# Dense sums of layers 2 and 3: three bf16 parts as one product of 512 columns and one of 256

## The reference, cut to what matters

```python
def _L1_gnn_ref(x, W1, b1, W2, b2, edge_index):
    loops = jnp.arange(n, dtype=edge_index.dtype)
    src = jnp.concatenate([edge_index[0], loops])
    dst = jnp.concatenate([edge_index[1], loops])
    deg = jax.ops.segment_sum(jnp.ones(src.shape[0], x.dtype), dst, num_segments=n)
    norm = dinv[src] * dinv[dst]                  # dinv = 1 / sqrt(deg)

    def gcn_conv(h, W, b):
        m = (h @ W)[src] * norm[:, None]
        return jax.ops.segment_sum(m, dst, num_segments=n) + b
    x1 = gcn_conv(x, W1, b1)
    x1 = x1 / jnp.maximum(jnp.linalg.norm(x1, axis=-1, keepdims=True), 1e-12)
    x2 = gcn_conv(x1, W2, b2)
    return x2 + x
```

## Time and profile before

| | us |
|---|---|
| median of 3 runs | 5319.24 |
| lowest and highest of them | 5316.11, 5332.93 |
| span of the profiled execution | 5305.9 |
| TensorE busy in it | 3977.3 (75%) |
| VectorE busy | 2919.9 (55%) |
| GpSimd busy | 2859.7 (54%) |
| ScalarE busy | 1417.2 (27%) |

### The profile page before, as it was taken

The page is one execution under the profiler, slowest core; times in us unless marked ns, Lnnn a source line. Parts: engine busy times, 40 slices in busy tenths (PEclk is TensorE's granted clock), DMA queues, the critical chain, the costliest instruction groups (busy, mean ns, idle before and its releaser), DMA issues.

```text
span 5305.9 us, 64097 instructions
## 1 busy us (share of the span) xinstructions
PE 3977.3 (75%) x20960; PEld 3151.6 (59%) x20961; DVE 2919.9 (55%) x7680; ACT 1417.2 (27%) x3894; POOL 2859.7 (54%) x3104
## 2 busy tenths in 40 slices
PE   6775655454555576777777996899996898886999
PEld 6653434343434455666666665787785777764666
DVE  7755655455546775555656556776665332243344
ACT  6603323232331222222222331333331000033221
POOL 7745566666656665565653002566565666643322
PEclk9857776777777777777777998999998999997999
DMA  3332343333333232222322002444444554444321
GB/s 92 106 70 78 110 112 100 98 99 99 97 95 90 86 87 79 81 85 81 86 81 66 25 14 74 130 144 144 138 146 140 160 155 138 138 136 135 103 80 54
DMA packets 337524, 535.23 MB, mean 101 GB/s; under 512 B 91587, under 2 KB 246452, under 8 KB 337186
## 3 DMA queue, kind: packets, MB, share of 16 engines
q0 software_dynamic: 133168, 361.15, 24.1%
q1 hardware_dynamic: 196902, 163.10, 10.0%
q10 hardware_dynamic: 7118, 6.83, 0.4%
HBM read 439.58 MB, written 94.26 MB: 101 GB/s over the span
## 4 chain that ended last, share of the span: by engine, by line
PE 54%; DVE 19%; issue 11%; another core or an unknown queue 11%; ACT 2%; DVEq 1%; POOL 1%; DMA 0%; ACTq 0%; SPq 0%; POOLq 0%
PE PSA L1091 15%; PE PSA L1239 12%; PE PSA L1486 4%; PE PSA L1472 4%; PE PSA L1248 4%; DVE ACC L2102 3%; PE PSA L1373 3%; PE PSA L1389 3%; DVE XIN L2075 2%; DVE XT L2075 2%; PE PSA L1041 1%; PE PSA L1219 1%; ACT ACC L1536 1%; DVE PSA L2066 1%
## 5 line engine op out<-in xcount | busy, mean ns | idle before, releaser
L915 POOL DMA_INDIRECT WORK<-tab,SRC x2504 | 2411.9, 963 | 1923.8 <-issue 666.6
L2102 DVE TENSOR_TENSOR ACC<-ACC,PSA 64x256 f32 x1296 | 541.9, 418 | 1221.2 <-remote 686.6
L1091 PE MATMUL PSA<-WORK,XIN 128*128 128x256 f32 x3032 | 881.2, 443 | 362.7 <-ACT XIN L1569 156.8
L1091 PEld LDWEIGHTS PSA<-WORK,XIN 128*128 128x128 f32 x3032 | 653.7, 225 | 490.5 <-issue 387.9
L1091 PE MATMUL PSA<-WORK,XT 128*128 128x256 f32 x1976 | 581.2, 446 | 217.8 <-ACT XT L1569 131.9
L1091 PEld LDWEIGHTS PSA<-WORK,XT 128*128 128x128 f32 x1976 | 427.7, 226 | 302.6 <-issue 226.4
L1239 PE MATMUL PSA<-WORK 128*128 128x256 bf16 x2730 | 367.0, 278 | 16.7 <-issue 16.5
L1239 PEld LDWEIGHTS PSA<-WORK 128*128 128x128 bf16 x2730 | 270.1, 100 | 60.7 <-issue 24.7
L2075 DVE TENSOR_TENSOR XIN<-PSA,DST 128x512 f32<-128x512 f32 x392 | 265.3, 679 | 3.9 <-issue 1.9
L1729 ACT ACTIVATE WORK<-PSA 128x512 bf16<-128x512 f32 x245 | 146.4, 598 | 428.1 <-PE PSA L1219 328.4
L1639 ACT ACTIVATE XIN<-XIN,HSB 128x128 f32<-128x128 f32 x504 | 160.2, 392 | 359.7 <-DVE XIN L2075 231.5
(11 more groups left out here) (511 smaller groups left out, 6768.4 us busy)
## 6 DMA issues: line engine op xcount, KB each, us to landing
WORK<-tab,SRC POOLq DMA_INDIRECT x2504
unit_counts_d<-WORK SPq DMA_DIRECT2D x245, 128.0 KB
WAX<-unit_counts_d SPq DMA_DIRECT2D x140, 128.0 KB
ACC<-in_L_ffn_w SPq DMA_DIRECT2D x16, 1024.0 KB
WORK<-unit_counts_d SPq DMA_DIRECT2D x105, 128.0 KB
tab<-WORK SPq DMA_DIRECT2D x98, 128.0 KB
slots_x<-FILL SPq DMA_DIRECT2D x4, 2080.0 KB
ACC<-slots_x SPq DMA_DIRECT2D x8, 910.0 KB
```

The lines of the kernel that those rows point to most:

```text
L915: po.indirect_dma_start(out=rows[:, 0:width], out_offset=None, in_=tab[:, :], in_offset=bass.IndirectOffsetOnAxis(ap=SRC[:, c:c + 1].bitca ...
L1091: last = pe.matmul(PS[h][:, 0:D], chosen[:, j * P:(j + 1) * P], rows[:, 0:D], start=(j == 0), stop=(j == Q - 1))
L2102: return ve.tensor_tensor(rows, rows, PS[h][half, 0:D], ALU.add)
```

## The change

`UNS` now names whole banks of 512 columns. In `sum_unit` the first two parts of a half, which stand side by side in SBUF (512 columns), are multiplied by one product into the whole bank, and the third part by a product of 256 columns that is summed onto the bank's first half. So a half takes two products in place of three, and the sums of a tile lie in two halves of a bank: parts 0 and 2 in the first, part 1 in the second. `add_tile` adds the second half to `ACC`, waits for that (`step` signals VectorE's own semaphore and `settle` waits for it), and then adds the first half.

```diff
-        UNS = [[PS[2][:, 0:D], PS[b][:, 0:D]] for b in (6, 5)]
+        UNS = [[PS[2], PS[b]] for b in (6, 5)]
...
-        def part_of(k, c):
-            first, held = [(t, v) for pieces in PIECES for t, n, _, v in pieces if t <= k < t + n][0]
-            return held[:, (k - first) * PD + c * D // 2:(k - first) * PD + (c + 1) * D // 2].bitcast(bf16)
+        def parts_of(k, c, n):
+            first, held = [(t, v) for pieces in PIECES for t, m, _, v in pieces if t <= k < t + m][0]
+            return held[:, (k - first) * PD + c * D // 2:(k - first) * PD + (c + n) * D // 2].bitcast(bf16)
...
                     for h in range(2):
-                        for c in range(C3):
-                            part = (v - 2 * n) * 2 + h
-                            last = pe.matmul(UNS[i][t % 2], UNC[i][n % len(UNC[i])][:, part * P:(part + 1) * P],
-                                             part_of(2 * u + h, c), start=(u == 0 and h == 0 and c == 0),
-                                             stop=(u == NL - 1 and h == 1 and c == C3 - 1))
+                        part = (v - 2 * n) * 2 + h
+                        counts = UNC[i][n % len(UNC[i])][:, part * P:(part + 1) * P]
+                        pe.matmul(UNS[i][t % 2], counts, parts_of(2 * u + h, 0, 2), start=(u == 0 and h == 0), stop=False)
+                        last = pe.matmul(UNS[i][t % 2][:, 0:D], counts, parts_of(2 * u + h, 2, 1), start=False,
+                                         stop=(u == NL - 1 and h == 1))
                 last.then_inc(s_ud, 1)
...
                 ve.wait_ge(s_ud, UNITS * i + last_unit(t) + 1)
-                ve.tensor_tensor(sums(t), sums(t), UNS[i][t % 2], ALU.add).then_inc(s_ut, 1)
+                step(ve.tensor_tensor(sums(t), sums(t), UNS[i][t % 2][:, D:2 * D], ALU.add))
+                settle()
+                ve.tensor_tensor(sums(t), sums(t), UNS[i][t % 2][:, 0:D], ALU.add).then_inc(s_ut, 1)
                 ve.wait_ge(s_ut, NT * i + t + 1)
```

## The result

The changed kernel takes 5375.84 us (median of 5 runs, 5338.59 to 5388.50), the kernel before beside it 5316.11 (5 runs): a ratio of 1.0101, 95% interval 1.0071 to 1.0131. I had forecast 5283 us. The profiled execution has a span of 5373.3 us, 67.4 us more than before's 5305.9.

A forecast was written before the change was run, and what follows sets the result against it. TensorE was taken to set the pace in layers 2 and 3. Columns -3.6, layer 3 stalls -34 and VectorE +1 summed to -36.6 us, giving 5283 us (chance 42%); the 8-in-10 range was 5230 to 5330 us.

The forecast's parts named there:

- The first step: Layers 2 and 3: TensorE, busy 650 of 725 and 585 of 655 us, sets the pace, so shortening its stream pays.
- it follows a TensorE that is up to 100 us faster: GpSimd in layer 3: its gathers wait 126 us for TensorE's side, so it would keep up with a faster TensorE.
- Columns: Dense sums, both layers: 1960 fewer products, 216.3 ns per 512 columns against two of 109.2 ns; taken as -3.6 us.
- Stalls of layer 3: TensorE in layer 3: fewer instructions remove 36% of 68.6 us of stalls and of 26 us lost clock; -34 us.
- instructions that arrive too slowly: Layer 3's dense products: supposed cause of TensorE's idle bursts without a semaphore, eight instructions arriving in 1.43 us.
- every instruction has the same chance: Layer 3: assumption that any TensorE instruction equally likely meets slow supply, leaving a share of 0.76 with fewer instructions.
- VectorE: Second addition in `add_tile`, about 0.5 us a tile, hidden by VectorE's waiting except at each layer's end; +1 us.
- the rival that made it late: Layer 2: the second addition delays one-hots for TensorE, costing 24.5 us, with layer 3's stalls unchanged; 5341 us, chance 6%.
- Layer 2's should move by 2 us or less: Expected sign: layer 2's stretch changes by at most 2 us, with TensorE's waits ahead of the count products unchanged.
- the 61 waits: Layer 2: 61 of 245 units followed by a count-product wait for copy or one-hot, losing a quarter of 2.05 us.
- The bursts move into layer 2 as well: Layer 2 catches stalls like layer 3's, costing 61 us, while layer 3 keeps its own; 5378 us, chance 7%.
- The stalls stay: Layer 3's stalls depend on time or other traffic, not instruction count; -2.6 us in all, 5317 us, chance 32%.

The follow-up runs named there:

- e8: Kernel before, with each gather of layers 2 and 3 replaced by a plain load of the same bytes from the same queue: 5123.18 us, ratio 0.9644.
- e15: Changed kernel with thirty small fills on GpSimd ahead of each group of four gathers in layer 2: 5296.67 us, ratio 0.9972.
- e16: Kernel before, with the third part's product of 256 columns split into two of 128, so four products a half: 5364.91 us, ratio 1.0112.
- e3: Changed kernel without VectorE's addition of the bank's second half, so the second part's sum is left out: 5359.25 us, ratio 1.0083.
- e4: Kernel before's three products of 256 columns, the second part's going into the bank's second half, with the changed kernel's two additions: 5322.07 us, ratio 1.0006.
- e13: Changed kernel, with the third part's product of 256 columns split into two of 128, so three products a half: 5301.19 us, ratio 0.9993.

## Why the prediction was wrong

**What sets the pace.** The first step failed: "in both layers TensorE sets the pace". TensorE's busy time of 90% does not show that. Without gathers (`e8`) the same TensorE stream runs layer 3 from its first dense product to its last in 549 us, where before took 662; and with more work on GpSimd (`e15`) the changed kernel got faster. I read the 126 us of GpSimd's waits as slack, "it follows a TensorE that is up to 100 us faster". They are pauses of a loop: GpSimd waits for TensorE's completions, and these often come late while gathers are out.

**Columns.** The size was right: 216 ns for 512 columns, 109 for the third part. With plain loads the two kernels take the same time.

**Stalls of layer 3.** The term -34 us is the one that carried the forecast, and it failed twice. The cause was not instructions that arrive too slowly (`e8`: none left, same pieces). And "every instruction has the same chance" does not hold: "issue" went from 68.6 to 67.0 us. Layer 3 did get shorter, by 10.2 us, and its clock rose to 0.98. That goes with longer rows of gathers (51 rather than 38 of seven or more) and fewer pauses; that the rows are the cause in this layer was not tested. The number of products does bear on this layer, since more of them cost 36 us (`e16`), but not by fewer waits named "issue".

**VectorE.** Right, and the rival that made it late fell. TensorE did wait longer for the one-hots, its sign, but without the second addition the loss stays (`e3`), and with the additions alone the ratio is 1.0006 (`e4`).

**Layer 2.** "Layer 2's should move by 2 us or less, with its waits ahead of L1219 unchanged" failed: it moved by 71 us, and the waits for the copy grew from 12.1 to 40.9 us. What the runs showed in its place is the loop of gathers and late completions, thrown out of its rhythm by two products a half in place of three. The hint stood in the earlier trace rows: waits of up to 4.7 us for ScalarE's copy, on an engine busy for 245 of 725 us, cannot come from the copy itself. I counted these waits and did not ask what the copy waited for. And 52 of the 61 waits that I put down to the copy or a one-hot end with "issue" in the earlier trace rows, 29.4 us: layer 2 stood still without a semaphore as well, only ahead of another product, so the two layers differed less than I thought.

**The rivals.** "The bursts move into layer 2 as well", at 7%, gave 5378 us and is nearest to 5376, but by another way: layer 3 did not keep its length, the waits named "issue" in layer 2 did not grow ahead of L1219 (29.4 to 27.0 us) and came to 0.9 us ahead of the dense products, and its price was borrowed from layer 3's. What it had right is that the two layers run the same products and that 1960 fewer could shift what follows. "The stalls stay" was right that fewer instructions leave the stalls of layer 3 as they are; they go with the gathers (`e8`). Its total was wrong, since it assumed a layer 2 that doesn't react.

**What stays open.** By which way the gathers hold up TensorE's completions, and whether TensorE also computes late then or only reports late, no run shows. That two products a half lengthen layer 2's rows of gathers is shown by `e13` against the changed kernel, and that these rows carry the loss by `e15`; why just two do so is not.

## What to carry over

An engine that is busy for 90% of a stretch need not set its pace. Where two engines wait for each other in turn, the waits are part of the pace and not slack: replace one side's work by something cheap (as in `e8`) before pricing a saving on the other. A saving on one side can lengthen the loop (after), and a pause on the other can shorten it (`e15`). A wait that ends with "remote" on a one-core kernel is a question: look at when the product was over and who got its completion when.

## What was unexpected of the hardware

- While GpSimd issues gathers one after another (0.95 us each, 0.30 us between), TensorE's completions often reach ScalarE, VectorE and GpSimd late; ScalarE's copies start up to 5.3 us behind the count products in before and 4.7 us in after, and several completions can arrive within 0.23 us. With plain loads from the same queue no copy starts over 0.04 us behind.
- The number of products can matter where their columns do not: splitting one product of 256 columns (109 ns) into two of 128 (112 ns together) cost 36 us in layer 3 of the kernel before, and the same split in the changed kernel took layer 2's gathers from 759.3 to 680.0 us. Two empty instructions a half changed nothing that stands out from the spread of layer 2.
- A fill of 128x1 on GpSimd has a mean of 106 ns by its rows, but fifty of them lengthened a pause by only 1.7 us, 34 ns each.
